# Scores and values of two units at once on parts of the array, in the second and third attention of a four-layer model

## The chip, the cores and the metric

The kernel runs on one core of a Trainium2 chip. The core has a matrix engine (TensorE, PE in the rows; PEld is its loading of weights), a vector engine (VectorE, DVE), an activation engine (ScalarE, ACT), a general engine (GpSimd, POOL) and a queue for transfers (SyncE, SP). Each takes its own instructions in order and waits on semaphores for the others. PE multiplies out of SBUF into PSUM, which has eight banks here; DVE and ACT read the banks. The metric is the device time of one execution in microseconds (us); lower is better.

## The reference

A model of four layers over 16 sequences of 102 tokens with 192 features. Each layer is an attention and a feed-forward part. The change touches the attention of the second layer (L1) and of the third (L2):

```python
def _attn(x, qkv_w, qkv_b, num_heads):          # second layer: 12 heads of 16
    ...
    scores = jnp.einsum('bqhd,bkhd->bhqk', q, k) * scale
    attn = jax.nn.softmax(scores, axis=-1)
    out = jnp.einsum('bhqk,bkhd->bqhd', attn, v)

def _L2_attn_ref(x, w_q, w_k, w_v, w_o, b_o):   # third layer: 12 heads of 64
    q = _split_heads(x @ w_q)
    k = _split_heads(x @ w_k)
    v = _split_heads(x @ w_v)
    scores = jnp.einsum('bhnd,bhmd->bhnm', q, k) / SCALE
    attn = jax.nn.softmax(scores, axis=-1)
    h = jnp.einsum('bhnm,bhmd->bhnd', attn, v)
    H = h.transpose(0, 2, 1, 3).reshape(x.shape[0], x.shape[1], HEADS * DIM_HEAD)
    out = H @ w_o + b_o
```

## The kernel before

All is float32. The 16 sequences are worked on in NG = 4 groups of GB = 4 sequences; each stage (an attention, a feed-forward part) is a loop over the groups. A group's attention consists of the projections of queries, keys and values (`product`, L1819), and then of UNITS = 16 units. A unit is three heads (HPU) of one sequence, so a sequence has UPB = 4 units.

A unit passes through the engines like this. PE multiplies queries and keys of three heads into one bank (scores, L1910). DVE takes the row minima (L917; the signs are turned, so they serve as maxima). ACT takes the exponentials of the three heads with their sums (L1604). DVE takes reciprocals of the sums (L923). POOL multiplies (L664, `probabilities`). PE transposes the three results into a bank (L1949). ACT copies them to SBUF (PT, L1598). PE multiplies them with the values (L1939) into a bank; once that bank holds half a sequence or a whole one, DVE copies it to OT (L933). PE multiplies OT with the output weights, in three parts that are spread over three steps (L1922), and DVE adds the result to the rows.

Nothing is scheduled at run time: each engine's order is written out as a loop over steps. On PE step s holds the scores of unit s, a part of a projection at `proj_step`, the values of unit s-5 and the transposes of unit s-3. On DVE step s holds the OT copy of unit s-6, the minima of unit s and the reciprocals of unit s-1. On ACT step s holds the copy of unit s-4 and the exponentials of unit s.

The keys lie in KZ, in a form made for whole-height products. A head has 16 or 64 features, and the three heads that share a tile's rows are told apart by zeros: KZ holds every key tile in four copies in the second attention (two in the third), each copy with one unit's rows filled and zeros elsewhere. ACT writes the filled parts (L1746, L1774, L1775). POOL writes the zeros with memsets, once ahead of each of these attentions (L748, L794), and PE waits for them (`halves_cleared`). In these two attentions three banks hold scores (0, 1 and 6), two hold transposes (TBANKS, 2 and 3), two hold values (4 and 7) and one the projection (PROJBANK, 5).

The first attention has relative positions (`pos`) and takes the same functions; it keeps its order.

Of the kernel before, what the change touches and what calls it, by code (L numbers as in the profile page):

```python
# [28 lines left out]
ACT = mybir.ActivationFunctionType  # L29
# [4 lines left out]
T = 102  # L34
# [113 lines left out]
def build(nc, t, out, scratch, flat, notes):  # L148
# [5 lines left out]
    with ctx:  # L154
# [231 lines left out]
        for r in range(YRING):  # L386
# [11 lines left out]

               "probs_in", "probs_ready",
               "sums_ready",  # L400
# [213 lines left out]
        def _(pool):  # L614
# [130 lines left out]
            powers(1)  # L745
            pool.wait_ge(sem["gated"], at.now("gated") + CT3)
            pool.wait_ge(sem["power_out"], at.now("power_out"))
# [42 lines left out]
            expert_rows(1)  # L790
            for r in range(YRING):
                pool.wait_ge(sem[f"scattered{r}"], 16 * len(range(r, TILES, YRING)))
            for half in range(2):
                pool.memset(KZ[64 - 64 * half:128 - 64 * half, half, :, :], 0.0  # L794
                            ).then_inc(sem["halves_cleared"], at.one("halves_cleared"))
            pool.wait_ge(sem["halves_cleared"], at.now("halves_cleared"))
            powers(1)
# [7 lines left out]
        def _(dve):  # L805
# [114 lines left out]
            def inverse_sums(n):  # L920
# [605 lines left out]
        def _(act):  # L1526
# [66 lines left out]
            def attention(pos=None):  # L1593
                for s in range(UNITS + (6 if pos else 4)):
                    if 0 <= s - 4 < UNITS:
                        k = at.bank(TBANKS)
                        src = full(k)[0:T, 0:TU].rearrange("p (h t) -> p h t", h=HPU)
                        free(activation(PT[s % 2][:, 0:HPU, :], src, ACT.Copy), k)  # L1598
                    if s < UNITS:
# [135 lines left out]
            with at.loop(act, NG) as g:  # L1735
# [5 lines left out]
                for j in range(3):  # L1741
                    k = at.bank(XBANKS)
                    src = full(k)[:, 0:TG]
# [22 lines left out]
            with at.loop(act, NG) as g:  # L1766
# [4 lines left out]
                for p in range(6):  # L1771
                    k = at.bank(XBANKS)
                    src = full(k)[:, 0:TG]
                    activation(KZ[0:64, 0, p, :], src[0:64], ACT.Copy)  # L1774
                    free(activation(KZ[64:128, 1, p, :], src[64:128], ACT.Copy), k)  # L1775
                attention()
# [19 lines left out]
        def _(pe):  # L1796
# [92 lines left out]
            def attention(per_tile, dv, wo, v_moved, pos=None):  # L1889
# [65 lines left out]
                if pos:  # L1955
                    at.one("exp_ready", UNITS)


# [255 lines left out]
            pe.wait_ge(sem["padded"], 1)  # L2214
            def zeros_there(n):
                pe.wait_ge(sem["halves_cleared"], at.take("halves_cleared", n))

            def convolution_in():
# [19 lines left out]
            convolution_out(1)  # L2238
            zeros_there(1)
            with at.loop(pe, NG) as g:  # L2240
# [6 lines left out]
                moved(*qk[-2:])  # L2247
                attention(4, 16, wp1, v_moved)
            with at.loop(pe, NG) as g:
# [114 lines left out]
            pe.wait_ge(sem["w2_loaded"], 16 * W2_LOADS)  # L2364
            pe.wait_ge(sem["halves_cleared"], at.take("halves_cleared", 2))
            with at.loop(pe, NG) as g:
# [11 lines left out]
                moved(*qk[-2:])  # L2378
                attention(2, 64, wo2, v_moved[-2:])

# [114 lines left out]
```

## Time and profile before

| what | us |
|---|---|
| time, median of 3 runs | 1702.41 |
| lowest and highest | 1700.49, 1703.29 |
| span of the profiled execution, first to last instruction | 1698.1 |
| PE busy in the span | 1444.5 (85%) |
| DVE, ACT, POOL busy | 683.9, 662.5, 384.9 |
| mean granted clock of TensorE | 0.900 of full speed |

The span is the profiled execution's own time as far as the page tells it; the median of the runs is 4.3 us longer, for what lies around the first and last instruction. The page's chain that ended last has 58% on PE and 12% on DVE; 8% of it is waiting for transfers, most of them the weights of the first layer's feed-forward part. In the chain a step is followed back from the last instruction to what released it. Where one engine's rows follow each other without a gap, that engine sets the pace.

### The profile page before, as it was taken

What the parts mean: (1) busy time and instruction counts of PE and PEld (TensorE: products, weight loads), DVE (VectorE), ACT (ScalarE), POOL (GpSimd) and SP (SyncE); (2) the same over time, 40 slices, a digit from 0 to 9 for tenths busy, and PEclk for the clock granted to TensorE, in tenths of its full rate; (3) what the DMA queues carried; (4) which work ended last, traced back from release to release, by engine and by line L of the source; (5) the groups of instructions that cost most, each with busy time, mean ns of one, the idle gap of its engine ahead of it and who ended that gap; (6) DMA issues with size and microseconds to landing.
All of it is one profiled execution on the core that took longest, in us unless ns stands there. A gap on an engine that the chain in (4) does not pass through costs nothing.

```text
span 1698.1 us, 31669 instructions
## 1 busy us (share of the span) xinstructions
PE 1444.5 (85%) x10300; PEld 1049.9 (62%) x10300; DVE 683.9 (40%) x2124; ACT 662.5 (39%) x2237; POOL 384.9 (23%) x464
## 2 busy tenths in 40 slices
PE   5899986796756778888899899699999999989994
PEld 3666664632212345666678799466765776789994
DVE  5557766511101376444423622433542423551113
ACT  1667663410000233777842122153663632213331
POOL 5212222300000122222200266220220200123441
PEclk8899996587778688999998899799999999889997
DMA  8434341679998400000003366200000200126553
GB/s 219 133 83 129 82 115 28 227 242 333 311 314 249 147 1 1 1 0 0 0 0 100 107 203 197 81 1 1 0 0 0 93 37 0 30 84 199 181 175 103
DMA packets 94439, 178.73 MB, mean 105 GB/s; under 512 B 35578, under 2 KB 54168, under 8 KB 92704
## 3 DMA queue, kind: packets, MB, share of 16 engines
q1 hardware_dynamic: 80144, 130.65, 26.1%
q10 hardware_dynamic: 7056, 30.67, 5.6%
q0 software_dynamic: 7136, 16.10, 3.1%
q8 instruction: 57, 0.93, 0.3%
q14 instruction: 46, 0.38, 0.1%
HBM read 150.39 MB, written 26.99 MB: 104 GB/s over the span
## 4 chain that ended last, share of the span: by engine, by line
PE 58%; issue 12%; DVE 12%; DMA 8%; ACT 6%; SPq 3%; POOL 1%; DVEq 0%; ACTq 0%; POOLq 0%
PE bank L1819 15%; DMA WM<-in_fc 7%; PE bank L2339 6%; PE bank L2325 4%; PE bank L1910 4%; PE bank L1922 3%; PE bank L1939 3%; PE bank L2329 3%; PE bank L1949 3%; PE bank L2000 2%; PE bank L1885 2%; PE bank L1992 2%; ACT ON L1604 2%; SPq L226 2%; PE bank L2256 1%
## 5 line engine op out<-in xcount | busy, mean ns | idle before, releaser
L1819 PE MATMUL bank<-XT,AREA 96*128 96x408 f32 (+1 forms) x640 | 239.1, 532 | 33.9 <-ACT XT L1558 16.6
L1819 PEld LDWEIGHTS bank<-XT,AREA 96*128 96x128 f32 (+1 forms) x640 | 122.1, 196 | 139.8 <-issue 99.8
L1910 PE MATMUL bank<-KZ,QT 128*102 128x102 f32 x1152 | 140.8, 262 | 9.0 <-ACT PB L1604 5.7
L664 POOL TENSOR_TENSOR PB<-PB,RCU 102x306 f32<-102x306 f32 x96 | 69.2, 720 | 318.5 <-DVE RCU L923 318.4
L648 POOL TENSOR_TENSOR RS<-VE,expo 102x4 f32<-102x4 f32 (+1 forms) x53 | 53.0, 1001 | 387.2 <-DVE VE L863 329.8
L1910 PEld LDWEIGHTS bank<-KZ,QT 128*102 128x102 f32 x1152 | 122.4, 174 | 27.2 <-issue 18.1
L2339 PE MATMUL bank<-WM,KZ 128*128 x660 | 118.2, 327 | 0.0
L2339 PEld LDWEIGHTS bank<-WM,KZ 128*128 128x128 f32 x660 | 105.7, 190 | 0.4
L1585 ACT ACTIVATE KZ<-bank,AREA 128x128 f32<-128x128 f32 x198 | 54.6, 374 | 121.8 <-PE bank L2329 121.8
L1922 PE MATMUL bank<-AREA,OT 128*102 128x192 f32 x384 | 88.9, 345 | 11.3 <-DVE SLOTS L1276 5.3
L1939 PE MATMUL bank<-PT,V 102*32 102x102 f32 (+1 forms) x1152 | 85.9, 270 | 14.5 <-DVE OT L933 12.3
L1598 ACT ACTIVATE PT<-bank 102x306 f32<-102x306 f32 x192 | 85.9, 449 | 26.2 <-PE bank L1949 25.8
L780 POOL DMA_INDIRECT rows_out<-KZ,TARGET x66 | 66.6, 1009 | 118.8 <-DVE KZ L1421 74.5
L1714 ACT ACTIVATE QT<-bank 128x512 f32<-128x512 f32 (+1 forms) x32 | 15.7, 490 | 196.2 <-PE bank L2134 196.2
L664 POOL TENSOR_TENSOR ON<-ON,RCU 102x306 f32<-102x306 f32 x96 | 67.0, 698 | 92.5 <-DVE RCU L923 92.2
L2325 PE MATMUL bank<-KZ,SLOTS 128*128 128x128 f32 x660 | 84.6, 275 | 2.6 <-issue 2.6
L1604 ACT ACTIVATE PB<-bank,MXU 102x102 f32<-102x102 f32 x192 | 65.5, 374 | 54.0 <-DVE MXU L917 54.0
L2325 PEld LDWEIGHTS bank<-KZ,SLOTS 128*128 128x128 f32 x660 | 82.0, 192 | 3.4 <-issue 3.4
L768 POOL DMA_INDIRECT KZ<-rows_in,TOKEN x66 | 67.5, 1023 | 53.0 <-DVE TOKEN L1398 33.5
L1556 ACT ACTIVATE XT<-bank 96x408 f32<-96x408 f32 x56 | 26.1, 501 | 136.9 <-PE bank L1837 127.8
L917 DVE TENSOR_REDUCE MXU<-bank 102x3 f32<-102x306 f32 x128 | 60.9, 476 | 43.0 <-PE bank L1910 38.9
L1214 DVE COPY QT<-bank 128x192 f32<-128x192 f32 x16 | 5.7, 357 | 177.7 <-PE bank L2144 177.7
(335 smaller groups left out, 2777.5 us busy)
## 6 DMA issues: line engine op xcount, KB each, us to landing
AREA<-in_fc SPq DMA_DIRECT2D x10, 1536.0 KB, 26.1
SLOTS<-in_m3w SPq DMA_DIRECT2D x33, 384.0 KB
WM<-in_fc ACTq DMA_DIRECT2D x5, 2304.0 KB, 19.5
WM<-in_fc SPq DMA_DIRECT2D x6, 1536.0 KB, 27.9
AREA<-in_fc ACTq DMA_DIRECT2D x4, 2304.0 KB, 20.6
SLOTS<-in_m1w SPq DMA_DIRECT2D x33, 256.0 KB
AREA<-pos_scratch SPq DMA_DIRECT2D x16, 459.0 KB
pos_scratch<-AREA SPq DMA_DIRECT2D x8, 913.5 KB
```

What stands on the lines that cost most here:

```text
L664: pool.tensor_tensor(p, p, scale, ALU.mult).then_inc(sem["probs_ready"], 1)
L768: pool.indirect_dma_start(XG[i % XRING], None, rows_in, bass.IndirectOffsetOnAxis(ap=TOKEN[:, i:i + 1], axis=0), bounds_check=NB * T - 1, ...
L780: pool.indirect_dma_start(rows_out, bass.IndirectOffsetOnAxis(ap=TARGET[:, i:i + 1], axis=0), YO[i % YRING], None, bounds_check=2 * NB * T ...
L917: give(dve.tensor_reduce(MXU[:, n % 4, 0:HPU], scores, AX.X, ALU.min), "probs_in")
L1598: free(activation(PT[s % 2][:, 0:HPU, :], src, ACT.Copy), k)
L1604: last = activation(p, p if pos else psum[k][0:T, cols(j)], ACT.Exp, scale=-1.0, bias=MXU[:, s % 4, j:j + 1], accum_out=SMU[:, s % 4, j:j ...
L1819: last = pe.matmul(dst, lhsT, rhs, start=n == 0, stop=n == len(pieces) - 1)
L1910: last = pe.matmul(psum[k][0:T, cols(j)], QT[:, tile, cols(bb)], KALL[:, unit % per_tile * (HEADS // per_tile) + tile, cols(bb)], start=Tr ...
L1922: last = pe.matmul(psum[PROJBANK][0:T, 0:D], OT[bb % 2][:, m, :], wo[:, m, :], start=m == 0, stop=m == parts - 1)
L1939: last = pe.matmul(psum[k][row:row + rows, cols(tile)], by_head(dv)[:, bb * HEADS + h, :], PT[n % 2][:, j, :], start=True, stop=True)
L2325: pe.matmul(p[:, c], w_all[:, (j * per + m) * 128:(j * per + m + 1) * 128], x[:, 0:TILE], start=m == 0, stop=False)
L2339: last = pe.matmul(p[:, 0:D], HG[i % HRING][:, f * 128:(f + 1) * 128], w2[:, bass.ds(e, 1), f * D:(f + 1) * D].rearrange("p o d -> p (o d) ...
```

## The change

In the second and third attention PE now takes a new function, `paired_attention`. Units s and s+1 are scored together in even steps: a head's queries and keys stand in 32 rows (second attention) or 64 (third), and the products of the two units run on different rows of the array, into two banks. The keys are therefore kept once (KT), without copies and zeros, and the memsets and waits for them go. The values of units s-6 and s-5 are multiplied together in even steps too, at the end of the step, on different columns of the array and into one bank. The transposes come first in each step. Those of even units go to bank 2, from which ACT copies as before; those of odd units go to bank 3, from which DVE copies (`odd_turns`, L922 of the kernel after). The copies go to four buffers in turn (PTS) instead of two. Scores have four banks now (0, 1, 6 and 7), values one (4).

```diff
-        SCORES, VALUES = (SBANKS + XBANKS[:1], SBANKS), (OBANKS[:1] + XBANKS[1:], OBANKS[:1])
+        SCORES, VALUES = (SBANKS + XBANKS, SBANKS), (OBANKS[:1], OBANKS[:1])
+        PTS = PT + [flat_ht[0:T, 4 * T * j:4 * T * (j + 1)].rearrange("p (h t) -> p h t", h=4) for j in range(2)]
...
-            pool.memset(KZ[:], 0.0).then_inc(sem["halves_cleared"], at.one("halves_cleared"))
-            pool.wait_ge(sem["halves_cleared"], at.now("halves_cleared"))
...
+            def odd_turns(n):
+
+                dve.wait_ge(sem["turn_ready"], at.take("turn_ready"))
+                src = psum[TBANKS[1]][0:T, 0:TU].rearrange("p (h t) -> p h t", h=HPU)
+                give(dve.tensor_copy(PTS[n % 4][:, 0:HPU, :], src), "turn_taken")
+                dve.wait_ge(sem["turn_taken"], at.now("turn_taken"))
...
                     if 0 <= s - 1 < UNITS:
                         inverse_sums(s - 1)
+                    if not pos and 0 <= s - 4 < UNITS and s % 2:
+                        odd_turns(s - 4)
...
-                    if 0 <= s - 4 < UNITS:
-                        k = at.bank(TBANKS)
+                    if 0 <= s - 4 < UNITS and (pos or s % 2 == 0):
+                        k = at.bank(TBANKS if pos else TBANKS[:1])
...
-                    for u in range(UPB):
-                        rows = slice(32 * u, 32 * u + 32)
-                        last = activation(KALL[rows, 3 * u + j, :], src[rows], ACT.Identity,
-                                          bias=bqk1[rows, 3 + j:4 + j])
-                    free(last, k)
+                    free(activation(KT[:, j, :], full(k)[:, 0:TG], ACT.Identity, bias=bqk1[:, 3 + j:4 + j]), k)
...
+                def turned(n):
+
+                    if n % 2:
+                        pe.wait_ge(sem["turn_taken"], turns_before + n // 2 + 1)
+                    else:
+                        moved(even_moved[n])
+
+                def turn(n):
+
+                    pe.wait_ge(sem["probs_ready"], at.take("probs_ready"))
+                    if n % 2:
+                        k = TBANKS[1]
+                        if n == 1:
+                            pe.wait_ge(sem[f"bank_free{k}"], at.now(f"bank_full{k}") + 1)
+                        else:
+                            turned(n - 2)
+                    else:
+                        k, p = claim(TBANKS[:1])
...
+                    for j in range(HPU):
+                        for unit in (s % UPB, s % UPB + 1):
+                            tile, row = unit // per_tile * HPU + j, unit % per_tile * rows_of
+                            rows = slice(row, row + rows_of)
+                            last = pe.matmul(psum[banks[bb * UPB % 4 + unit]][0:T, cols(j)], QT[rows, tile, cols(bb)],
+                                             KT[rows, tile, cols(bb)], start=True, stop=True)
...
+                for s in range(STEPS):
+                    if 0 <= s - 3 < UNITS:
+                        turn(s - 3)
...
+                    if s < UNITS and s % 2 == 0:
+                        scores(s)
+                    if 0 <= s - 6 < UNITS and s % 2 == 0:
+                        values(s - 6)
```

PE in the second attention, before: one step's transposes, the next step's scores and values (banks are told by the waits; ON and PB are the four buffers of probabilities).

```order
L1949 MATMUL bank<-ident,ON 102x102 [waits bank_free2,probs_ready]
L1949 MATMUL bank<-ident,ON 102x102 x2
L1907 REGISTER_ALU
L1910 MATMUL bank<-KZ,QT 102x102 [waits exp_ready]
L1910 MATMUL bank<-KZ,QT 102x102 x2
L1813 REGISTER_ALU
L1939 MATMUL bank<-PT,V 32x102 [waits bank_free3]
L1939 MATMUL bank<-PT,V 32x102 x2
```

The same place now: the transposes of an even and of an odd unit, then the scores of a pair and its values.

```order
L1973 REGISTER_ALU
L1796 REGISTER_ALU [waits probs_ready]
L1983 MATMUL bank<-ident,PB 102x102 [waits bank_free2]
L1983 MATMUL bank<-ident,PB 102x102 x2
L1973 REGISTER_ALU
L1967 REGISTER_ALU [waits probs_ready]
L1983 MATMUL bank<-ident,PB 102x102 [waits turn_taken]
L1983 MATMUL bank<-ident,PB 102x102 x2
L1997 REGISTER_ALU
L2003 MATMUL bank<-KZ,QT 102x102 [waits exp_ready]
L2003 MATMUL bank<-KZ,QT 102x102 x5
L2020 MATMUL bank<-KZ,V 32x102 [waits turn_taken,bank_free2]
```

The scores of a pair stand behind the transposes of two units, the second of which wait for `turn_taken`, DVE's signal; before, a unit's scores stood behind transposes that waited for ACT and POOL alone.

DVE in the second attention, before (L917 are minima, L923 reciprocals):

```order
L923 RECIPROCAL RCU<-SMU 102x3 [waits exp_ready,probs_in]
L917 TENSOR_REDUCE MXU<-bank 102x3 [waits scores_ready,sums_ready]
L918 REGISTER_ALU
L923 RECIPROCAL RCU<-SMU 102x3 [waits exp_ready,probs_in]
L917 TENSOR_REDUCE MXU<-bank 102x3 [waits scores_ready,sums_ready]
```

And now, over two steps (L909 are minima, L915 reciprocals, L922 the copy of an odd unit):

```order
L909 TENSOR_REDUCE MXU<-bank 102x3 [waits scores_ready,turn_taken]
L910 REGISTER_ALU
L915 RECIPROCAL RCU<-SMU 102x3 [waits exp_ready,probs_in]
L909 TENSOR_REDUCE MXU<-bank 102x3 [waits scores_ready,sums_ready]
L910 REGISTER_ALU
L915 RECIPROCAL RCU<-SMU 102x3 [waits exp_ready,probs_in]
L920 REGISTER_ALU [waits sums_ready]
L922 COPY KZ<-bank 102x306 [waits turn_ready]
```

The copy stands in every second step, behind that step's reciprocals, which wait for ACT's exponentials (`exp_ready`).

## Rows read from the trace of the kernel before

**Rows 1.** Windows, second attention: stretch, length, busy PE PEld DVE ACT POOL, clock.

```profile
757.00:800.00 43.00, 37.39 (x312) 26.29 (x311) 18.89 (x58) 32.95 (x130) 12.15 (x17) 1.00 0.00 0
```

**Rows 2.** Chain of waits, a group of the second attention: start, us, what.

```profile
758.76 5.65 PE bank L1819 x16
...
766.89 4.24 PE bank L1819 x20
...
778.33 0.54 PE bank L1910 x6
...
779.62 0.54 PE bank L1910 x6
```

**Rows 3.** Chain of waits, third attention: values, a third of a projection.

```profile
1198.96 0.49 PE bank L1939 x6
...
1200.40 0.65 PE bank L1922 x4
```

**Rows 4.** Timeline, same group: start, us, engine, line, operation, shapes, [idle before].

```profile
771.80 1.83 PE L1910 MATMUL bank<-KZ,QT 128*102 128x102 f32 x18 [0.67 <-issue]
772.59 1.07 DVE L917 TENSOR_REDUCE MXU<-bank 102x3 f32<-102x306 f32 x2 [0.80 <-PE bank L1910]
773.10 0.35 ACT L1604 ACTIVATE PB<-bank,MXU 102x102 f32<-102x102 f32 x1 [1.40 <-DVE MXU L917]
...
774.29 0.18 DVE L923 RECIPROCAL RCU<-SMU 102x3 f32<-102x3 f32 x1 [0.63 <-ACT PB L1604]
...
775.27 0.17 DVE L923 RECIPROCAL RCU<-SMU 102x3 f32<-102x3 f32 x1 [0.20 <-ACT PB L1604]
...
775.57 0.48 DVE L917 TENSOR_REDUCE MXU<-bank 102x3 f32<-102x306 f32 x1
...
776.35 0.47 PE L1949 MATMUL bank<-ident,PB 102*102 102x102 f32 x3
...
776.66 0.70 PE L1910 MATMUL bank<-KZ,QT 128*102 128x102 f32 x6
...
797.88 0.48 DVE L933 COPY OT<-bank 128x306 f32<-128x306 f32 x1 [2.83 <-PE bank L1939]
...
798.92 1.23 PE L1922 MATMUL bank<-AREA,OT 128*102 128x192 f32 x6 [1.10 <-DVE SLOTS L1276]
```

**Rows 5.** Timeline, one group of the third attention.

```profile
1187.24 1.78 PE L1910 MATMUL bank<-KZ,QT 128*102 128x102 f32 x18
...
1219.49 2.20 PE L1922 MATMUL bank<-AREA,OT 128*102 128x192 f32 x12 [1.08 <-DVE H L1483]
```

**Rows 6.** Timeline, experts of the second layer, whole and half height.

```profile
1072.11 1.05 PE L2325 MATMUL bank<-KZ,SLOTS 128*128 128x128 f32 x8
...
1073.10 0.72 PE L2329 MATMUL bank<-KZ,SLOTS 64*128 64x128 f32 x8
...
1073.74 0.43 PE L2339 MATMUL bank<-WM,KZ 128*128 x1
```

**Rows 7.** Timeline, ahead of the second attention, and the same normalization later.

```profile
662.02 5.24 DVE L867 TENSOR_SCALAR XN<-SLOTS,MV,RS 102x192 f32<-102x192 f32 x4 [1.12 <-POOL RS L648]
662.10 4.18 POOL L748 MEMSET KZ<- 128x4896 f32 x1
...
761.22 1.25 DVE L867 TENSOR_SCALAR XN<-SLOTS,MV,RS 102x192 f32 x4 [1.21 <-POOL RS L648]
```

**Rows 8.** Chain of waits, first group's projections.

```profile
669.81 8.00 PE bank L1819 x16
```

**Rows 9.** Windows, first attention, two neighbouring stretches.

```profile
121.42:124.84 3.42, 1.99 (x16) 1.59 (x14) 1.13 (x3) 3.40 (x16) 0.70 (x1) 1.00 0.00 0
124.84:128.25 3.41, 3.41 (x18) 2.80 (x17) 2.71 (x12) 2.38 (x10) 0.70 (x1) 0.50 0.00 0
```

**Rows 10.** Timeline, first attention, at the low clock.

```profile
62.90 1.26 PE L1910 MATMUL bank<-KZ,QT 128*102 128x102 f32 x6
...
64.25 0.48 DVE L911 TENSOR_TENSOR PB<-bank,AREA 102x306 f32<-102x306 f32 x1 [0.41 <-DVE V L956]
```

More of the change, by code:

```diff
@@ L790, in _ @@
             expert_rows(1)
[L791 to L796, printed above, removed]
             powers(1)
@@ L1772, in _ @@
                     k = at.bank(XBANKS)
-                    src = full(k)[:, 0:TG]
-                    activation(KZ[0:64, 0, p, :], src[0:64], ACT.Copy)
-                    free(activation(KZ[64:128, 1, p, :], src[64:128], ACT.Copy), k)
+                    free(activation(KT[:, p, :], full(k)[:, 0:TG], ACT.Copy), k)
                 attention()
@@ L1956, in attention, with paired_attention, values_taken, scores @@
                     at.one("exp_ready", UNITS)
+            def paired_attention(per_tile, dv, wo, v_moved):
+                banks, values_bank = SCORES[False], VALUES[False][0]
+                parts, rows_of = (3 if dv == 16 else 6), 128 // per_tile
+                values_before, turns_before = at.now("values_taken"), at.now("turn_taken")
+                even_moved = {}
+                def values_taken(f):
+                    pe.wait_ge(sem["values_taken"], values_before + f + 1)
+                def turned(n):
[14 more added lines that the diff above has]
+                    for j in range(HPU):
+                        last = pe.transpose(psum[k][0:T, cols(j)], PB[n % 4][:, j, :], ident[0:T, 0:T])
+                    if n % 2:
+                        last.then_inc(sem["turn_ready"], at.one("turn_ready"))
+                    else:
+                        even_moved[n] = filled(last, k)
+                def scores(s):
+                    for k in (banks[s % 4], banks[s % 4 + 1]):
+                        if s < 4:
+                            pe.wait_ge(sem[f"bank_free{k}"], at.now(f"bank_full{k}") + 1)
+                        else:
+                            at.one("exp_ready")
+                    if s >= 4:
+                        pe.wait_ge(sem["exp_ready"], at.now("exp_ready"))
+                    bb = s // UPB
+                    for j in range(HPU):
+                        for unit in (s % UPB, s % UPB + 1):
[3 more added lines that the diff above has]
+                                             KT[rows, tile, cols(bb)], start=True, stop=True)
+                            if j == HPU - 1:
+                                last.then_inc(sem["scores_ready"], at.one("scores_ready"))
+                def values(n):
+                    f = fill_of(dv, n)
+                    if n == 0:
+                        moved(*v_moved)
+                    turned(n)
+                    turned(n + 1)
+                    if f >= 1 and n % (UPB // fills(dv)) == 0:
+                        values_taken(f - 1)
+                    for unit in (n, n + 1):
+                        for j in range(HPU):
+                            row, rows, tile, _ = av_place(dv, HPU * (unit % UPB) + j)
+                            last = pe.matmul(psum[values_bank][row:row + rows, cols(tile)],
+                                             by_head(dv)[:, unit // UPB * HEADS + HPU * (unit % UPB) + j, :],
+                                             PTS[unit % 4][:, j, :], start=True, stop=True)
+                    if av_filled(dv, (n + 1) % UPB):
+                        last.then_inc(sem["values_ready"], 1)
+                for s in range(STEPS):
+                    if 0 <= s - 3 < UNITS:
+                        turn(s - 3)
+                    for bb in range(GB):
+                        for i in range(3):
+                            if s != proj_step(bb, i):
+                                continue
+                            if i == 0:
+                                values_taken(fills(dv) * (bb + 1) - 1)
+                                k, p = claim(None, PROJBANK)
+                            for m in range(i * parts // 3, (i + 1) * parts // 3):
+                                last = pe.matmul(psum[PROJBANK][0:T, 0:D], OT[bb % 2][:, m, :], wo[:, m, :],
+                                                 start=m == 0, stop=m == parts - 1)
+                            if i == 2:
+                                filled(last, PROJBANK)
+                    if s < UNITS and s % 2 == 0:
+                        scores(s)
+                    if 0 <= s - 6 < UNITS and s % 2 == 0:
+                        values(s - 6)
+                at.one("values_taken", fills(dv) * GB)
+                at.one("turn_taken", UNITS // 2)
+                at.one("exp_ready", len(banks))
@@ L2247, in _ @@
                 moved(*qk[-2:])
[L2248 removed]
+                paired_attention(4, 16, wp1, v_moved)
             with at.loop(pe, NG) as g:
```

13 lines of the change are left out of this document (3 added, 10 removed).

## The prediction, made before the changed kernel ran

> **What bounds the kernel now.** I read the granted clock and busy shares of the two attentions first, then the chain of waits through one group of each, then the timeline of one group's first units for the handoffs from engine to engine. In the second attention the clock is granted at full speed (2.4 GHz) and PE is busy 37.39 of 43.00 us, ACT 32.95 [rows 1]: PE sets the pace, ACT is close behind. The chain shows PE handing over to PE: the scores of one unit start at 778.33, those of the next at 779.62, a pitch of 1.29 us, 0.54 of it scores [rows 2]. Two other places count. In the projections of a group PE works from 758.76 for 5.65 us, then stands still until 766.89 because ACT writes every key tile four times, and the first scores start at 771.80 [rows 2, 4]. And ahead of the first group POOL clears KZ for 4.18 us while DVE's normalization beside it takes 5.24 us instead of 1.25 [rows 7].
>
> From first scores to the start of a group's last projection the second attention takes 798.92 - 771.80 = 27.1 us [rows 4], the third 1219.49 - 1187.24 = 32.25 [rows 5]. These two spans are what the change has to shorten, four times each.
>
> **The change part by part.**
>
> Keys kept once, second attention. ACT's 12 quarter copies become 3 whole ones, no longer than the queries'. PE's work of 5.65 + 4.24 us then runs without a stop, some 10.0 us with a handoff, where 771.80 - 758.76 = 13.05 stand now: -3.05 a group, -12.2 in all. In the third attention PE's projections already run through, so halving ACT's copies is worth nothing there.
>
> The clearing. Without it DVE's normalization takes 1.25 instead of 5.24 us: -4.0. PE also idles less, and the first 16 projections, 8.00 us at a low clock [rows 8] against 5.65 in a later group [rows 2], lose 2.35. Together -6.4. The clearing ahead of the third attention stands beside a wait for DMA rows and counts zero; if it did slow something, it is a gain of some us at most.
>
> Paired scores and values. Twelve half-height score instructions replace two times six. The nearest rows are the experts' 64-row products: eight whole ones fill 1072.11 to 1073.10, 0.99 us, eight paired ones 1073.10 to 1073.74, 0.64 [rows 6]. So a pair of units takes 1.08 x 0.64/0.99 = 0.70 us where one unit takes 0.54. The bounds are 0.54 (perfect overlap) and 1.08 (none); I take 0.70, as the rows are the same kind of pair. PE thus gets much cheaper. What decides is what it then waits for.
>
> The new wait. Transposes of odd units go to one bank that only DVE empties. PE's transposes of odd unit n wait until DVE has copied unit n-2. DVE's copy of unit n-2 stands behind the reciprocal of unit n+1, and that one waits for the exponentials of n+1. Unit n+1 is the first of the pair scored just before; behind the transposes, in PE's order, stand the projection and the next pair's scores. So no pair is scored until the pair before has gone through DVE, ACT and DVE again. One turn of this ring, start of scores to start of scores, from [rows 4]:
> scores to minimum, 772.59 - 771.80 = 0.79, plus 0.16 for the pair: 0.95;
> minimum to exponentials, 773.10 - 772.59: 0.51;
> exponentials to reciprocal, 774.29 - 773.10: 1.19;
> reciprocal to DVE's next instruction, 775.57 - 775.27: 0.30;
> DVE's copy out of PSUM, as its 128x306 copy at 797.88: 0.48, and a handoff of 0.05 (estimated from the 0.03 to 0.05 between neighbours in these rows);
> transposes to scores, 776.66 - 776.35: 0.31, and 0.10 for the change of array shape (the 0.99 in [rows 6] is that much more than eight times 0.111).
> Sum 3.89, say 3.9 us a pair, against two units at 1.29 now. Of this PE works about 1.9, ACT 2.3 and DVE 2.3 at most: none is the bound, the ring is.
>
> A group, second attention. The first two pairs need no wait. Pair 2 starts behind the transposes of unit 1: 0.95 + 0.51 + 1.19 + 0.98 (775.27 - 774.29, one unit more) + 1.08 (reciprocal through POOL to transposes, 776.35 - 775.27) + 0.31 + 0.10 = 5.1. Five turns of 3.9 bring pair 7 to 24.6. Steps 10, 12 and 14 put a third of a projection ahead of the scores, half of 0.65 each [rows 3], so 25.6. The tail: 3.5 to the transposes of unit 13, 1.05 to those of 15 (one more DVE copy), then transposes, three projection thirds and two value pairs, 2.3, a handoff of 0.5, and 1.04 from the copy at 797.88 to the projection at 798.92: 8.4. Sum 34.0, +6.9 over 27.1, +27.6 for four groups.
>
> A group, third attention. The same 24.6, with three thirds of 0.65 [rows 3]: 26.5. The tail is longer, since every value pair is copied by DVE ahead of the odd copy and a value unit takes 0.49 [rows 3], some 0.7 for a pair: 3.5 + 3.05 + 3.05 + 0.3 + 1.04 = 10.9. Sum 37.4, +5.15 over 32.25, +20.6.
>
> The clock. Six scores take 1.26 us at the low level [rows 10] and 0.70 at the high one [rows 4]; scores to minimum takes 64.25 - 62.90 = 1.35 instead of 0.79. With transposes scaled alike a turn costs 0.56 + 0.25 = 0.8 more when the clock is low. In the first attention it fell once in a stretch after PE had been busy 1.99 of 3.42 us; the next stretch was granted 0.50 [rows 9]. PE will be idle about half of each turn, and has least to do in the second attention. I charge half of the turns and the tail there, 3.5 us a group, and 1.5 a group in the third, where scores and projections are bigger: +20. The bounds are 0 and all turns low, 6.3 and 9.2 a group: +62.
>
> Zero: one bank for values instead of two (its wait ends within a turn), and two more buffers in HT, idle then.
>
> **Sum.** -12.2 - 6.4 + 27.6 + 20.6 + 20 = +49.6 on the profiled span of 1698.1: 1748. The median of the runs, 1702.4, lies 4.3 above the span; with the same 4.3 I predict 1752 us.
>
> The Trainium skill (TensorEngine Tiling (Array Packing), PSUM Bottleneck) says that tiling speeds up TensorE only, and that copies out of PSUM may then become the limit, to be shared by ScalarE and VectorE. By it the pace would be ACT's share, and sharing the copies would pay; the first rival below gives that time. No row here shows it yet, since ACT's work now fits beside PE's.
>
> **Rivals.**
> 1. Faster: the copy on DVE is not in the way, because it comes out of its queue before the next transposes need it. The pair is then paced by ACT: two units of 0.98 and one copy of 0.3, 2.3 us, with the projections in PE's gaps. Against 2.58 plus 1.0 or 2.0 of projections per two pairs this saves about 5 us a group in the second and 8 in the third: 1702 - 18.6 - 52 = 1632. If the reciprocal behind the next pair's minimum still holds (0.51 + 1.08 + 0.31 + 0.10 + 0.95 = 2.95 a pair), the attentions come out nearly level and 1687 is left. For it speaks that DVE and ACT have room; against it the order of the two queues. It decides if the copy of unit n-2 does not stand behind the reciprocal of n+1. 4% for 1687, 3% for 1632.
> 2. The clock stays up in both attentions: 1752 - 20 = 1732. For it: gaps of a turn are under 2 us, and now the clock holds at 1.00 [rows 1]. Against: it fell in the first attention, where PE also waits in turns [rows 9]. 25%.
> 3. The clock stays low in nearly all turns: 1752 + 42 = 1794. 9%.
> 4. Pairs do not overlap in the array: scores to minimum grows by 0.38 more, 40 turns, +15: 1768 or so. Against it [rows 6]. 7%.
>
> **How the numbers follow.** The forecast, ring of 3.9 with the clock partly low, has 50%, no change 2%. The predicted time is its 1752. From 1732 less half a turn's error (0.25 us on 40 turns, 10 us) the range starts at 1722; upward it takes in rival 4 and part of rival 3, to 1782. What this measurement can tell from no change is 0.2%, about 3.4 us. Faster: 3 + 4 = 7%; same: 2%, as a few turns shorter than I think would land there; slower: the rest, 91%.
>
> **What would show it.** PE's transposes of odd units waiting for DVE's copy (some 1 to 2 us, seven times a group); scores of pairs 3.9 us apart, more where the clock is low; PE's busy share in 43 us falling to around half; ACT waiting for minima; the normalization ahead of the second attention at 1.25 us; a group's projections at 10 us. I am wrong if the pitch of pairs is near 2.3 or 3.0, or if PE is still the bound.

## The result, and the profile after

The changed kernel takes 1804.82 us (median of 4 runs, 1798.35 to 1821.87) against 1701.45 for the kernel before. The ratio on record, which is not quite the quotient of the two medians, is 1.064, with a 95% interval of 1.0579 to 1.0701. I had forecast slower, 1752, in a range that ended at 1782. The sign and the wait were right; the loss is 103 us where I had 50.

The windows of the two attentions, from a group's first scores to its last projection (columns as in [rows 1]; the first row is of the second attention, the other of the third):

```profile
674.24:717.97 43.73, 32.55 (x259) 22.10 (x258) 17.84 (x49) 20.70 (x105) 11.16 (x16) 0.57 0.01 1
...
1252.84:1297.40 44.56, 31.50 (x278) 23.70 (x277) 19.68 (x52) 21.00 (x105) 11.16 (x16) 0.77 0.00 0
```

Before, these stretches took 27.1 and 32.25 us [rows 4, 5], at a clock of 1.00 [rows 1]. Now they take 43.73 and 44.56, and no engine is busy throughout. The granted clock, 0.57 and 0.77, is a mean of the two levels, 0.50 (1.2 GHz) and 1.00 (2.4 GHz): the low one holds in 0.43/0.50 = 86% of the first stretch and 46% of the second. In another group of the second attention one sees when it fell:

```profile
733.38:736.79 3.41, 0.76 (x6) 0.53 (x6) 1.96 (x6) 3.41 (x21) 1.42 (x3) 1.00 0.00 0
736.80:774.32 37.52, 30.45 (x230) 20.73 (x228) 13.95 (x38) 17.20 (x85) 9.73 (x14) 0.50 0.00 0
```

PE had waited for the group's first units and been busy 0.76 of 3.41 us. Then the clock stayed low for 37.52 us, nearly to the end of the group, whose last projection starts at 775.66.

One turn of the ring, scores to scores, in the timeline of the second attention (L2003 scores, L909 minima, L1605 exponentials, L915 reciprocals, L922 the copy, L1983 transposes; columns as in [rows 4]):

```profile
741.65 1.36 PE L2003 MATMUL bank<-KZ,QT 32*102 32x102 f32 x12
...
743.11 0.47 DVE L909 TENSOR_REDUCE MXU<-bank 102x3 f32<-102x306 f32 x1 [2.20 <-PE bank L2003]
...
743.62 0.35 ACT L1605 ACTIVATE ON<-bank,MXU 102x102 f32<-102x102 f32 x1 [2.29 <-DVE MXU L909]
...
744.81 0.18 DVE L915 RECIPROCAL RCU<-SMU 102x3 f32<-102x3 f32 x1 [0.51 <-ACT ON L1605]
...
745.11 0.48 DVE L922 COPY KZ<-bank 102x306 f32<-102x306 f32 x1
...
745.64 0.75 PE L1983 MATMUL bank<-ident,PB 102*102 102x102 f32 x3 [1.13 <-DVE KZ L922]
746.32 1.36 PE L2003 MATMUL bank<-KZ,QT 32*102 32x102 f32 x12
```

It is the chain of the forecast, step by step, in 746.32 - 741.65 = 4.67 us. PE stands 1.13 us for VectorE's copy, every engine waits for the one before, and PE's own steps take 1.36 and 0.75 us, as at the low clock.

Ahead of the second attention (L859 is the normalization, L1813 the products):

```profile
659.95 1.25 DVE L859 TENSOR_SCALAR XN<-SLOTS,MV,RS 102x192 f32<-102x192 f32 x4 [1.12 <-POOL RS L649]
...
663.29 8.46 PE L1813 MATMUL bank<-XT,AREA 96*128 96x408 f32 x24 [1.05 <-ACT XT L1559]
...
671.58 2.77 PE L1813 MATMUL bank<-AREA,XT 96*102 96x192 f32 x16
...
674.28 1.06 PE L2003 MATMUL bank<-KZ,QT 32*102 32x102 f32 x24
```

The normalization takes 1.25 instead of 5.24 us [rows 7]. The products run without a stop, 674.28 - 663.29 = 10.99 us to the first scores where 13.05 stood. So the savings came.

### The profile page after: what moved, and what is told of

It reads as the page before. It is cut to its first block, busy times and chain, and to the rows that moved or that the text cites. A ratio compares the mean times of both kernels' runs of the same rounds, so it can differ in the third digit from the quotient of the medians.

```text
span 1796.6 us, 31565 instructions
## 1 busy us (share of the span) xinstructions
PE 1474.5 (82%) x10300; PEld 1059.1 (59%) x10300; DVE 710.5 (40%) x2188; ACT 611.6 (34%) x2113; POOL 377.1 (21%) x461
## 4 chain that ended last, share of the span: by engine, by line
PE 38%; issue 32%; DVE 12%; DMA 8%; POOL 4%; ACT 3%; SPq 2%; DVEq 0%; POOLq 0%; ACTq 0%
DMA WM<-in_fc 7%; PE bank L2426 6%; PE bank L1813 5%; PE bank L2412 4%; PE bank L2416 3%; DVE MXU L909 2%; PE bank L2091 2%; PE bank L2003 2%; POOL PB L665 1%; PE bank L2083 1%; SPq L226 1%; PE bank L2343 1%; PE bank L1904 1%; POOL ON L665 1%; PE bank L2037 1%
## 5 line engine op out<-in xcount | busy, mean ns | idle before, releaser
L1813 PE MATMUL bank<-XT,AREA 96*128 96x408 f32 (+1 forms) x640 | 238.4, 532 | 28.2 <-ACT XT L1559 15.5
L1813 PEld LDWEIGHTS bank<-XT,AREA 96*128 96x128 f32 (+1 forms) x640 | 123.6, 196 | 132.2 <-issue 106.4
L909 DVE TENSOR_REDUCE MXU<-bank 102x3 f32<-102x306 f32 x128 | 60.9, 476 | 118.5 <-PE bank L2003 113.6
L1605 ACT ACTIVATE PB<-bank,MXU 102x102 f32<-102x102 f32 x192 | 63.9, 347 | 107.2 <-DVE MXU L909 107.0
L2037 PE MATMUL bank<-AREA,OT 128*102 128x192 f32 x288 | 81.3, 416 | 9.0 <-DVE H L1484 4.5
L1605 ACT ACTIVATE ON<-bank,MXU 102x102 f32<-102x102 f32 x192 | 63.8, 349 | 72.9 <-DVE MXU L909 72.8
L1983 PE MATMUL bank<-ident,ON 102*102 102x102 f32 x192 | 43.4, 357 | 43.1 <-DVE PT L922 42.9
L1983 PE MATMUL bank<-ident,PB 102*102 102x102 f32 x192 | 40.0, 333 | 43.2 <-POOL PB L665 23.0
L2003 PE MATMUL bank<-KZ,QT 32*102 32x102 f32 (+1 forms) x768 | 70.6, 346 | 0.0
```

The source lines that it names most:

```text
L909: give(dve.tensor_reduce(MXU[:, n % 4, 0:HPU], scores, AX.X, ALU.min), "probs_in")
L1605: last = activation(p, p if pos else psum[k][0:T, cols(j)], ACT.Exp, scale=-1.0, bias=MXU[:, s % 4, j:j + 1], accum_out=SMU[:, s % 4, j:j ...
L1813: last = pe.matmul(dst, lhsT, rhs, start=n == 0, stop=n == len(pieces) - 1)
L1983: last = pe.transpose(psum[k][0:T, cols(j)], PB[n % 4][:, j, :], ident[0:T, 0:T])
L2003: last = pe.matmul(psum[banks[bb * UPB % 4 + unit]][0:T, cols(j)], QT[rows, tile, cols(bb)], KT[rows, tile, cols(bb)], start=True, stop=True)
L2037: last = pe.matmul(psum[PROJBANK][0:T, 0:D], OT[bb % 2][:, m, :], wo[:, m, :], start=m == 0, stop=m == parts - 1)
```

## The experiments

All times are medians, with the ratio on record to the kernel before, run on the same chip, and its 95% interval. In the cuts of code `...` stands for lines left out. The question was first how much of the loss is the ring and how much the clock, and then why the clock was low so much longer than I had charged.

**Holding the clock with added work.** Both kernels add whole products to the changed kernel, in a bank that PE holds anyway; nobody reads them. The first adds ten behind the transposes of an even unit:

```
                     if 0 <= s - 3 < UNITS:
                         turn(s - 3)
+                        for _ in range(10 if s % 2 else 0):
+                            pe.matmul(psum[SCORES[False][(s - 3) % 4]][:, 0:128], ident[:], ident[:], start=True, stop=True)
```

> The changed kernel with ten whole 128x128 products ahead of every second step's end (behind the transposes of an even unit, ahead of the wait for VectorE's copy), whose results nobody reads. In the changed kernel pairs of scores start 4.7 us apart without a projection and 5.4 with one, all at the low clock. Theory A (the time lost beyond the forecast is the clock): the granted clock in the second attention goes from about 0.5 to above 0.9, pairs start 3.9 to 4.1 us apart, and the run takes 1745 to 1770 us. Theory B (the handoffs between engines are simply longer than I read, whatever the clock): pairs stay 4.7 us apart or grow by what the products take, 1800 to 1850 us.

1787.88 us, 1.0515 (1.0456 to 1.0575): neither theory's time. The clock did rise as theory A had it, to 0.92 in the window of one group, and in the second attention pairs without a projection start 3.7 to 4.1 us apart, near theory A's 3.9 to 4.1. The timeline says why the time did not follow (L2030 are the added products, two instructions each):

```profile
734.84:775.90 41.06, 38.48 (x419) 34.27 (x418) 17.00 (x47) 20.68 (x105) 11.16 (x16) 0.92 0.00 0
```

```profile
749.41 2.42 PE L2030 MATMUL bank<-ident 128*128 128x128 f32 x20
751.66 0.43 PE L1983 MATMUL bank<-ident,PB 102*102 102x102 f32 x3
752.02 0.79 PE L2003 MATMUL bank<-KZ,QT 32*102 32x102 f32 x12
```

The ten took 2.42 us and PE is busy 38.48 of 41.06 us: the experiment replaced one bound by another. The second has four of them, and eight ahead of the first transposes.

> The changed kernel with whole 128x128 products whose results nobody reads: eight ahead of a group's first transposes and four behind the transposes of every even unit. In the run with ten they took 0.24 us each, 2.42 in all, so PE was nearly full with them and the pitch of 3.8 us there may be PE's own. Four take 0.97, which with PE's 1.9 us a pair leaves room. Theory A (the ring is 3.9 us at the full clock, the rest of the loss was the clock): granted clock above 0.9 in both attentions, pairs without a projection 3.8 to 4.0 us apart, 1745 to 1765 us. Theory B (my ring was too long, and at the full clock it is well shorter): pairs 3.2 to 3.5 us apart, 1715 to 1740 us. Theory C (four do not hold the clock): 1785 us or more.

1748.45 us, 1.0233 (1.017 to 1.0297), theory A. Its windows, in two groups of the second attention and one of the third:

```profile
693.63:729.20 35.57, 28.73 (x339) 22.79 (x338) 17.85 (x49) 20.69 (x105) 11.15 (x16) 1.00 0.01 2
743.34:780.28 36.94, 31.44 (x339) 25.62 (x338) 17.85 (x49) 20.68 (x105) 11.15 (x16) 0.91 0.00 0
1229.47:1268.17 38.70, 33.68 (x358) 27.89 (x357) 19.69 (x52) 21.01 (x105) 11.15 (x16) 1.00 0.00 0
```

And one turn at the full clock, in its timeline:

```profile
748.45 0.79 PE L2003 MATMUL bank<-KZ,QT 32*102 32x102 f32 x12
...
751.35 0.48 DVE L922 COPY PT<-bank 102x306 f32<-102x306 f32 x1
...
751.88 0.47 PE L1983 MATMUL bank<-ident,ON 102*102 102x102 f32 x3 [1.32 <-DVE PT L922]
752.28 0.78 PE L2003 MATMUL bank<-KZ,QT 32*102 32x102 f32 x12
753.00 0.60 PE L2020 MATMUL bank<-PT,V 102*32 102x102 f32 x12
```

The ring is 752.28 - 748.45 = 3.83 us at the full clock, with PE waiting 1.32 for the copy. More work on PE made the kernel 56 us faster than the changed one.

**Shortening the ring.** VectorE's copy ahead of the minima, or all copies on ScalarE:

```
+                    if not pos and 0 <= s - 4 < UNITS and s % 2:
+                        odd_turns(s - 4)
                     if s < UNITS:
                         minima(s, pos)
                     if 0 <= s - 1 < UNITS:
                         inverse_sums(s - 1)
-                    if not pos and 0 <= s - 4 < UNITS and s % 2:
-                        odd_turns(s - 4)
```

> The changed kernel with VectorE's copy of unit s-4 moved ahead of the minima and reciprocals of its step. Theory A (a ring through minimum, exponentials, reciprocal and VectorE's copy paces the pairs): without the exponentials of the pair before in the ring, a turn loses about 0.95 us (2.95 instead of 3.9 at the full clock, 3.75 instead of 4.7 at the low one); 56 turns, some 50 us, 1745 to 1765 us. Theory B (at the low clock PE's own work, 1.36 + 0.90 + 2 x 0.75 = 3.8 us a pair and a projection's third, is nearly the bound, or the probabilities of the same unit come as late as the copy): gains under 20 us, 1785 to 1805.

1762.06 us, 1.0365 (1.031 to 1.0419): theory A. Its timeline, still at the low clock, has pairs 750.71 - 746.98 = 3.73 us apart, and in these turns PE's transposes no longer wait for VectorE but for POOL's probabilities, as theory B had allowed (in later turns of the group, with a third of a projection, they wait for VectorE's copy again, 0.54 us at 754.12):

```profile
746.98 1.36 PE L2003 MATMUL bank<-KZ,QT 32*102 32x102 f32 x12
...
750.03 0.75 PE L1983 MATMUL bank<-ident,PB 102*102 102x102 f32 x3 [0.18 <-POOL PB L665]
750.71 1.36 PE L2003 MATMUL bank<-KZ,QT 32*102 32x102 f32 x12
```

```
-                    if 0 <= s - 4 < UNITS and (pos or s % 2 == 0):
-                        k = at.bank(TBANKS if pos else TBANKS[:1])
+                    if 0 <= s - 4 < UNITS:
+                        k = at.bank(TBANKS)
...
```

ScalarE copies every unit here, and `odd_turns` goes from VectorE's order.

> The changed kernel with all copies of transposes on ScalarE again (two banks and four buffers, paired scores and values stay). Theory A (the ring): ScalarE's copy of unit n-2 stands behind the exponentials of unit n+1, so the ring stays, shorter by the reciprocal and the wait for the end of the sums, about 0.5 us a turn: pairs some 4.1 to 4.2 us apart, 1770 to 1785 us. Theory B (the copy on VectorE is what costs): the attentions come back to the time before, some 1685 to 1705 us.

1756.34 us, 1.0374 (1.0299 to 1.0448). Theory B falls. In the timeline a turn without a projection takes 743.43 - 739.32 = 4.11 us, as theory A had it, and the transposes (L1971) wait for ScalarE's copy:

```profile
739.32 1.36 PE L1988 MATMUL bank<-KZ,QT 32*102 32x102 f32 x12
...
742.75 0.75 PE L1971 MATMUL bank<-ident,PB 102*102 102x102 f32 x3 [0.57 <-ACT KZ L1597]
743.43 1.36 PE L1988 MATMUL bank<-KZ,QT 32*102 32x102 f32 x12
```

The time is below theory A's 1770, though. I had counted the turns alone. The tail of a group, where VectorE's copies go away too, may be shorter, but in the third attention the clock is also higher than in the changed kernel (0.82 against 0.77, in a group of 37.57 us); which of the two it is was not shown.

**Taking the ring away.** The scores of a pair go ahead of the transposes of s-3, with eight buffers of probabilities:

```
+                    if s < UNITS and s % 2 == 0:
+                        scores(s)
                     if 0 <= s - 3 < UNITS:
                         turn(s - 3)
...
-                    if s < UNITS and s % 2 == 0:
-                        scores(s)
```

> The changed kernel with the scores of a pair ahead of the transposes of unit s-3 in PE's step, which needs eight buffers of probabilities instead of four. The wait for VectorE's copy then stands behind the scores, so a pair waits for the pair before the last. Theory A (the ring is the cause, the clock follows from PE's idle time in it): pairs 2.3 to 2.6 us apart, clock above 0.9, 1650 to 1700 us. Theory C (the clock also falls because the products use parts of the array; at the low clock PE's own work of some 3.8 us a pair, 4.5 with a third of a projection, is the bound): clock 0.5 to 0.7 in the second attention, pairs 3.6 to 3.9 apart, 1735 to 1765 us.

1745.76 us, 1.0258 (1.0189 to 1.0327): theory C. The timeline shows PE without a gap, pairs 736.77 - 733.29 = 3.48 us apart, at the low clock:

```profile
733.29 1.36 PE L2004 MATMUL bank<-KZ,QT 32*102 32x102 f32 x12
734.58 0.75 PE L1984 MATMUL bank<-ident,KZ 102*102 102x102 f32 x3
...
736.77 1.36 PE L2004 MATMUL bank<-KZ,QT 32*102 32x102 f32 x12
```

```profile
733.29:741.53 8.24, 8.24 (x65) 5.80 (x64) 4.31 (x12) 5.70 (x30) 3.23 (x5) 0.50 0.00 0
```

So waiting alone does not explain the low clock: in this window PE is busy 8.24 of 8.24 us at 0.50, and its steps are as long as before.

**The rows of the products.** First the kernel before with keys kept once, but units scored one by one in the old order (`rows` are the 32 or 64 of the unit; the first attention keeps its whole products; ScalarE's copies and the clearing, cut here, change as in the changed kernel):

```
-                            last = pe.matmul(psum[k][0:T, cols(j)], QT[:, tile, cols(bb)],
-                                             KALL[:, unit % per_tile * (HEADS // per_tile) + tile, cols(bb)],
-                                             start=True, stop=True)
...
+                            last = pe.matmul(psum[k][0:T, cols(j)], QT[rows, tile, cols(bb)],
+                                             KT[rows, tile, cols(bb)], start=True, stop=True)
```

> The kernel before with keys kept once and no clearing: scores and values of one unit at a time in the old order, but each score product uses only the 32 or 64 rows of its unit. Theory A (the parts of my sum hold, and the clock follows how long PE is busy): 4 x 3.05 + 6.4 = 18.6 us less than before, 1678 to 1688 us, clock near 1.0 in the second attention. Theory C (the clock follows how much of the array works, so products on a quarter of the rows let it fall): granted clock in the second attention well under 1.0, and 1700 us or more.

1854.78 us, 1.0912 (1.0832 to 1.0991): theory C. In a group of its second attention the granted clock is 0.56, with PE busy 42.55 of 45.20 us; the parts of my sum alone would have made it faster. To take ScalarE's copies and the clearing out of the question, one edit on PE of the kernel before, everything else kept:

```
-                            last = pe.matmul(psum[k][0:T, cols(j)], QT[:, tile, cols(bb)],
-                                             KALL[:, unit % per_tile * (HEADS // per_tile) + tile, cols(bb)],
+                            last = pe.matmul(psum[k][0:T, cols(j)], QT[rows, tile, cols(bb)],
+                                             KALL[rows, unit % per_tile * (HEADS // per_tile) + tile, cols(bb)],
```

Here too `rows` are those of the unit, and the whole height in the first attention.

> The kernel before with one edit on PE: each score product of the second and third attention reads only the 32 or 64 rows that belong to its unit, from the same copies with zeros; copies, clearing, order and instruction counts stay. Theory C (products on a part of the rows let the clock fall by themselves): clock near 0.6 in the attentions, a unit about 2.46 us apart in the second, and 1845 to 1885 us. Theory B (the clock or the time of the kernel with keys kept once came from ScalarE's shorter copies or the missing clearing): 1695 to 1712 us, as before.

1874.73 us, 1.1002 (1.09 to 1.1104): theory C. The windows are one behind the last scores of a group of the second attention, two neighbours in the next group, and one of the third attention; then come two units in the timeline (L1912 scores, L1941 values, L1951 transposes):

```profile
726.31:735.70 9.39, 9.39 (x59) 4.98 (x58) 1.66 (x5) 4.08 (x11) 1.39 (x2) 0.50 0.00 0
...
758.46:761.86 3.40, 1.89 (x23) 1.42 (x19) 2.02 (x6) 2.71 (x17) 0.97 (x2) 1.00 0.00 0
761.87:800.00 38.13, 38.13 (x217) 25.32 (x217) 10.54 (x32) 19.98 (x96) 10.15 (x15) 0.50 0.00 0
...
1311.42:1352.36 40.94, 40.94 (x196) 30.52 (x197) 11.06 (x33) 18.81 (x93) 10.07 (x15) 0.50 0.00 0
```

```profile
786.14 1.36 PE L1912 MATMUL bank<-KZ,QT 32*102 32x102 f32 x6
787.43 0.56 PE L1941 MATMUL bank<-PT,V 102*32 102x102 f32 x6
787.92 0.75 PE L1951 MATMUL bank<-ident,ON 102*102 102x102 f32 x3
788.60 1.36 PE L1912 MATMUL bank<-KZ,QT 32*102 32x102 f32 x6
```

PE is busy 38.13 of 38.13 us and granted 0.50, and in the third attention 40.94 of 40.94. The same instructions with 128 rows, 96 or 64 of them zeros in the copies, were granted 1.00. In the kernel before, the units of one group, and in its first attention a stretch at the low clock ([rows 9]) with the one behind it:

```profile
775.00:798.00 23.00, 21.88 (x235) 15.52 (x234) 11.14 (x35) 20.74 (x103) 10.70 (x16) 1.00 0.00 0
...
124.84:128.25 3.41, 3.41 (x18) 2.80 (x17) 2.71 (x12) 2.38 (x10) 0.70 (x1) 0.50 0.00 0
128.25:131.66 3.41, 2.89 (x26) 2.27 (x25) 2.45 (x9) 2.39 (x10) 1.87 (x3) 1.00 0.75 223
```

So two things have to be told apart. The fall itself came behind a stretch in which PE was idle, 1.89 busy of 3.40 us, much like the 1.99 of 3.42 in [rows 9]. PE waits there for the group's first units, 1.16 us for ScalarE's exponentials where the kernel before, with longer first scores, waits 0.61 and keeps its clock. What differs is what follows the fall. In the first attention, with whole-height scores (and other products beside them), the clock was back after 3.41 us of work; with the rows cut it stayed low through 38.13 us without a gap. A unit goes from 1.29 to 788.60 - 786.14 = 2.46 us. The first window holds no score product at all, only values (32 columns), transposes and output projections, and the clock stays at 0.50 there too.

The reverse: the kernel with keys once, and two whole products ahead of each unit's scores.

```
+                        for _ in range(0 if pos else 2):
+                            pe.matmul(psum[k][:, 0:128], ident[:], ident[:], start=True, stop=True)
                         for j in range(HPU):
                             tile = unit // per_tile * HPU + j
```

> The kernel before with keys kept once and no clearing, scores of one unit on its own rows, and two whole 128x128 products that nobody reads ahead of every unit's scores: 0.48 us more of PE's work a unit. Theory C (products on a part of the rows let the clock fall, and nothing else made that kernel slow): the clock is back near 1.0, a unit takes 1.29 + 0.48 = 1.77 us instead of 2.46, and the run takes 1702 - 19 + 128 x 0.48 = 1745 us (1730 to 1760), over 90 us less than without the added work. Theory B (products on a part of the rows are slow for another reason): 1855 + 60 = 1915 us.

Its four runs took 1753.45 to 1790.76 us (median 1786.87), too unlike for a ratio, but all of them at least 64 us under the 1854.78 without the added work: theory C in its direction, though only the shortest run reaches its 1730 to 1760. Without the added work PE had no gaps there either (27.00 busy of 27.00 us in a window at 0.50), so it is not more busy time that brings the clock back. The profiled run, the one of 1790.76, has three groups of the second attention as in the first of these windows, and the fourth as in the second; the last two windows show the fall in the fourth:

```profile
784.91:820.70 35.79, 34.53 (x319) 26.04 (x318) 13.70 (x41) 24.11 (x113) 11.14 (x16) 1.00 0.00 0
835.26:894.60 59.34, 58.29 (x320) 43.15 (x319) 13.78 (x41) 24.65 (x113) 11.13 (x16) 0.53 0.00 0
...
835.20:838.60 3.40, 3.40 (x28) 2.87 (x26) 1.55 (x5) 1.68 (x10) 0.14 (x1) 1.00 0.00 0
838.62:842.02 3.40, 3.40 (x17) 2.94 (x16) 1.30 (x4) 1.79 (x11) 1.24 (x2) 0.50 0.01 2
```

One program, the same instructions, 35.79 us or 59.34, and the granted clock beside each. In the fourth group PE was busy 3.40 of 3.40 us ahead of the fall, with scores on 32 rows and added whole products in turn. So here, once, the clock fell without idle time.

Six score instructions of one unit on 32 rows, in a group at the full clock, for comparison with the twelve of a pair above:

```profile
794.01 0.78 PE L1901 MATMUL bank<-KZ,QT 32*102 32x102 f32 x6
794.72 0.38 PE L1929 MATMUL bank<-PT,V 102*32 102x102 f32 x6
```

**Ring and clock together.** Scores first, the copy early, and then without added products, or with eight ahead of the first transposes and two or one behind those of every even unit.

> The kernel with scores ahead of the transposes and VectorE's copy ahead of the minima, without any added products: what the added products in the run that took 1687.9 us were worth. Theory C (products on parts of the array let the clock fall; the added whole ones hold it): clock 0.5 to 0.8 in the second attention, pairs 3.5 us apart or more in most turns, 1725 to 1750 us. Theory A (once the ring is gone PE is busy enough and the added products are only cost): clock above 0.9 there, 1665 to 1690 us.

> Scores ahead of the transposes as in the run before, VectorE's copy ahead of the minima, and whole products that nobody reads (eight ahead of a group's first transposes, two behind those of every even unit, 0.48 us). Theory A with C (ring and clock together are the whole loss): pairs 2.4 to 2.9 us apart at a clock above 0.9, 1650 to 1695 us, faster than the kernel before. Rival (another wait follows at once, of ScalarE or of the projections): 1700 to 1740 us.

> The same with eight whole products ahead of a group's first transposes and one, not two, behind those of every even unit. Theory C with one enough: clock 1.00 in both attentions, 0.24 us less of PE's work in some seven turns of each of eight groups, up to 13 us: 1675 to 1686 us. One too few: clock below 0.9 in places and 1690 to 1740 us. PE not the bound there: 1686 to 1690.

Without: 1726.09 us, 1.0135 (1.0072 to 1.0198), theory C. With two: 1687.9 us, 0.9893 (0.9847 to 0.9938), theories A and C. With one: 1686.55 us, 0.9879 (0.9833 to 0.9925), within 1 us of the border between "one enough" and "PE not the bound"; the times with one and with two cannot be told apart. One added product is enough to keep the clock at 1.00. Their windows, second and third attention; without (the lowest clock of its four groups in the second, the others have 0.73 to 0.78):

```profile
726.50:760.80 34.30, 29.32 (x259) 20.54 (x258) 17.84 (x49) 20.74 (x105) 11.14 (x16) 0.65 0.00 0
1200.58:1236.88 36.30, 30.27 (x277) 22.89 (x276) 19.69 (x52) 20.52 (x105) 11.13 (x16) 0.81 0.00 0
```

with two:

```profile
723.77:752.07 28.30, 25.20 (x307) 19.34 (x306) 17.85 (x49) 20.68 (x105) 11.15 (x16) 1.00 0.00 0
1177.44:1210.48 33.04, 30.00 (x326) 24.37 (x325) 19.68 (x52) 20.56 (x105) 11.15 (x16) 1.00 0.00 0
```

and with one:

```profile
717.65:745.45 27.80, 23.48 (x292) 17.56 (x291) 17.86 (x49) 20.42 (x105) 11.14 (x16) 1.00 0.00 0
1173.92:1206.22 32.30, 28.44 (x310) 22.52 (x309) 19.69 (x52) 20.41 (x105) 11.14 (x16) 1.00 0.00 0
```

These two take about 1% less than the kernel before. But their attentions take 27.8 to 28.3 and 32.3 to 33.0 us, no less than before the change (27.1 and 32.25). By their profiled spans, 1689.4 and 1686.2 us against 1698.1, they gain 8.7 and 11.9 us, less than the keys and the clearing save (next section); the pairs on parts of the array, with the work that holds their clock, give nothing back here.

## Why the prediction was wrong, step by step

The profiled spans differ by 1796.6 - 1698.1 = 98.5 us; the forecast had +49.6. (The 4.3 us that I added on top were too many: the profiled run of the changed kernel took 1798.35 - 1796.6 = 1.75 us more than its span. That matters little here.)

- **Keys and clearing.** Forecast -12.2 and -6.4. Measured 10.99 - 13.05 = -2.06 a group, -8.2; the normalization as forecast, and the first group's products run like a later group's. Some -15 instead of -18.6: I had put the products at 10.0 us, and they take 11.0 even without a stop.
- **The cost of a pair.** Right: forecast 0.70 us for the twelve score instructions; in the kernel with four added products the next step starts 753.00 - 752.28 = 0.72 behind. Six unpaired ones on 32 rows take 794.72 - 794.01 = 0.71 to the next step, and at the low clock both take 1.36, so the pairs overlap wholly. Rival 4 falls.
- **The ring.** Right: forecast 3.9 at the full clock, measured 3.83; forecast 0.8 more at the low one, measured 4.67 - 3.83 = 0.84. Moving the copy or the scores shortens or removes it, as the ring's steps say. Rival 1 falls, since the copy stands where the order has it.
- **A group at the full clock.** Forecast 34.0 and 37.4 us. Measured with the four added products, which I can't take out of it: 35.57 and 38.70. Against 27.1 and 32.25 this is +8.5 and +6.5 a group, +60, where I had +48.2. Up to the scores of the last pair the second attention was as forecast, 719.39 - 693.63 = 25.8 against 25.6; the rest of the 35.57, the tail, takes 9.8 where I had 8.4.
- **The clock.** This step failed: "I charge half of the turns and the tail there, 3.5 us a group, and 1.5 a group in the third", +20. Measured 43.73 - 35.57 = 8.2 and 44.56 - 38.70 = 5.9 a group, +56. Rival 3 ("the clock stays low in nearly all turns", 1794, 9%) is what happened in the second attention, where the low clock holds in 86% of the stretch; in the third it holds in 46%.

Together -15 + 60 + 56 = +101, against 98.5 measured. The term that was mis-sized is the clock's, by 36 of the missing 49 us. Behind the size stands a wrong step. From [rows 9] I took the clock to fall after idle time of PE, and to stay low for a part of the turns. The fall is mostly as I read it: in the changed kernel it comes after PE was busy 0.76 of 3.41 us (one fall above came without idle time). What I had wrong is that it comes back when PE works again. The kernel with the single edit shows that with scores on 32 or 64 rows the clock stays at 0.50 while PE is busy 38.13 of 38.13 us. Before the change every score product had 128 rows, most of them zeros, and no row that I had read from that trace shows what fewer do to the clock. That the low clock in the changed kernel is held by the cut rows is carried over from the kernels with the single edit and with scores first; there PE does not wait, while in the changed kernel it does, 30.45 busy of 37.52 us. The ring with whole-height products was not run, so the share of the waiting in the low clock is not told apart.

The price of a low turn was right for a turn without a projection (0.84), too small for one with a third of it (5.45 against 4.28 us in the first of them), and the bound of +62 for low turns throughout holds for the sum, but not for each attention: 8.2 a group against 6.3 in the second, 5.9 against 9.2 in the third. I gave that case 9% where the change itself cut the rows of every score product.

The rule of the Trainium skill that I had weighed (TensorEngine Tiling (Array Packing), PSUM Bottleneck: tiling speeds up TensorE only, and the copies out of PSUM may become the limit) is not borne out as a limit on the engines that copy: with ring and clock out of the way, ScalarE is busy 20.68 and VectorE 17.85 of 28.30 us, and PE 25.20. A copy out of PSUM did stand in the way, but by its place in VectorE's order: it takes 0.48 us, and moving it ahead brought 1804.82 us to 1762.06. Some waiting for copies is left, too: with one added product PE's transposes wait 5.8 us for ScalarE's copies and 1.6 for VectorE's, over the four groups of the second attention.

Two things stay open. Whether the values' products, which have 32 or 64 columns before and after, hold the clock low by themselves was not tried; the window without scores above (0.50 at 9.39 busy of 9.39 us) speaks for it in the second attention, while the kernel before ran the same products at 1.00. And why one group of the kernel with keys once and added work fell to the low clock, and three did not, I can't tell from its trace: PE was not idle ahead of the fall.

## What to carry to other kernels

Zeros that fill up a product's rows can be worth their time: before cutting products to the rows they need, try the cut alone, look at how long the granted clock stays low after a wait, and weigh a few whole products in PE's idle time. When a copy moves to another engine, write down what stands ahead of it in that engine's order and follow it back to the next product; a ring that closes there sets the pace, whatever the engines' shares say. And where two causes come together, take away one at a time: with the scores first and the copy early it took 1726.09 us, with the clock held 1748.45, with both 1687.9.

## What the runs showed of the hardware that I had not expected

- With the same score products on 32 and 64 rows instead of 128 the granted clock, once it had fallen after idle time, stayed at 0.50 with PE busy 38.13 of 38.13 us, and the kernel went from 1695.91 to 1874.73 us. In the first attention, with scores on 128 rows, it had come back after 3.41 us.
- The same instructions ran at 1.00 in three groups of one execution (35.79 us) and at 0.53 in the fourth (59.34 us), where the clock fell while PE was busy 3.40 of 3.40 us.
- Twelve score instructions of two units on different rows take 0.72 us to the next step, as long as six of one unit on its rows (0.71).
- A whole 128x128 product of this type, two instructions, takes 0.24 us at the full clock (ten in 2.42).
